# Flamingo block in one kernel: the softmax probabilities turned by VectorE and regrouped through memory in place of TensorE's transposes

## The reference

```python
x = x + jnp.tanh(g_xattn[0]) * _L0_xattn_ref(_layernorm(x, axis=-1), ctx_4096, ctx_4096, L0_xattn_Wq, L0_xattn_Wk, L0_xattn_Wv, L0_xattn_Wd)
x = x + jnp.tanh(g_ffn[0]) * _L0_ffn_ref(_layernorm(x, axis=-1), ...)
```

```python
scores = jnp.einsum('bhqd,bhkd->bhqk', queries, keys) * scale
scores = jnp.where(causal[None, None], scores, jnp.finfo(scores.dtype).min)
attn = jax.nn.softmax(scores, axis=-1)
ctx = jnp.einsum('bhqk,bhkd->bhqd', attn, values)
ctx = ctx.transpose(0, 2, 1, 3).reshape(B, Sq, NHEADS * HEAD_DIM)
return ctx @ Wd.T
```

## Time and profile before

| what | value |
|---|---|
| time, median of 3 runs | 1545.78 us (1545.67 to 1546.14) |
| the profiled execution's own time | 1548.8 us |
| its span | 1547.0 us |
| PE busy | 1480.5 us, 96% of the span |
| VectorE, ScalarE, GpSimd busy | 64%, 35%, 40% |
| chain that ended last, by engine | PE 82%, VectorE 7%, ScalarE 3%, GpSimd 3%, DMA 2% |
| a group in the middle | 79.86 us |

### The profile page before, as it was taken

One profiled execution on the slowest core, in us unless ns is written; L12 is line 12 of the kernel. 1 busy time (PEld: TensorE's weight loads), 2 busy tenths in 40 slices (PEclk: granted clock), 3 DMA queues, 4 the chain that ended last, 5 costly groups with the idle time before them and its releaser, 6 DMA issues.

```text
span 1547.0 us, 19240 instructions
## 1 busy us (share of the span) xinstructions
PE 1480.5 (96%) x7488; PEld 1214.2 (78%) x7488; DVE 990.7 (64%) x1536; ACT 537.4 (35%) x829; POOL 624.5 (40%) x403
## 2 busy tenths in 40 slices
PE   7899999999999999999999999999999999968996
PEld 7878888888888888877778888888888888855553
DVE  4956565656565656565675656464656565678995
ACT  4424131414141413144341414141413132317883
POOL 2534243434343333330443434343333333225996
PEclk9999999999999999999999999999999999998998
DMA  8823131313222222217341313121212221193553
GB/s 275 251 59 101 36 97 28 93 40 78 54 75 56 76 56 68 64 58 251 89 138 32 87 28 83 35 77 42 75 43 73 45 59 32 44 287 108 188 177 136
DMA packets 193786, 142.92 MB, mean 92 GB/s; under 512 B 147744, under 2 KB 162592, under 8 KB 193312
## 3 DMA queue, kind: packets, MB, share of 16 engines
q1 hardware_dynamic: 193264, 138.54, 31.5%
q0 software_dynamic: 432, 3.15, 1.0%
HBM read 124.88 MB, written 19.92 MB: 94 GB/s over the span
## 4 chain that ended last, share of the span: by engine, by line
PE 82%; DVE 7%; ACT 3%; POOL 3%; DMA 2%; issue 1%; SPq 1%; POOLq 0%; ACTq 0%
PE psum L511 16%; PE psum L513 16%; PE psum L512 16%; PE psum L565 7%; PE psum L600 7%; PE psum L601 7%; PE psum L602 7%; POOL go L1180 2%; PE psum L574 2%; DVE stat L1252 1%; DVE sc L1551 1%; ACT xg L1050 1%; ACT xu L1051 1%; DVE xt_lo L1208 1%; ACT xi L1055 1%
## 5 line engine op out<-in xcount | busy, mean ns | idle before, releaser
L511 PE MATMUL psum<-xt_hi,wq_hi 128*128 128x512 f32 x1024 | 405.2, 396 | 2.0 <-DVE xt_lo L1208 2.0
L513 PE MATMUL psum<-xt_hi,wq_lo 128*128 128x512 f32 x1024 | 400.1, 391 | 0.0
L512 PE MATMUL psum<-xt_lo,wq_hi 128*128 128x512 f32 x1024 | 399.4, 390 | 0.0
L1112 POOL TENSOR_TENSOR rot<-rot 128x1024 f32<-128x1024 f32 x64 | 153.5, 2399 | 430.7 <-DVE rot L1312 429.0
L1360 DVE TENSOR_TENSOR acc<-psum,acc 128x512 f32<-128x512 f32 x256 | 175.8, 688 | 164.7 <-PE psum L602 162.6
L1084 POOL TENSOR_TENSOR wd_lo<-wd_raw,wd_hi 128x512 fp32r<-128x512 f32 x128 | 164.3, 1290 | 244.6 <-ACT wd_hi L857 244.6
L511 PEld LDWEIGHTS psum<-xt_hi,wq_hi 128*128 128x128 f32 x1024 | 192.9, 188 | 41.1 <-DVE xt_lo L1208 2.8
L513 PEld LDWEIGHTS psum<-xt_hi,wq_lo 128*128 128x128 f32 x1024 | 192.5, 188 | 40.8
L512 PEld LDWEIGHTS psum<-xt_lo,wq_hi 128*128 128x128 f32 x1024 | 193.0, 188 | 38.3
L893 ACT ACTIVATE vw_hi<-psum 64x512 fp32r<-64x512 f32 x256 | 151.3, 591 | 203.6 <-PE psum L513 200.4
L1084 POOL TENSOR_TENSOR wq_lo<-wq_raw,wq_hi 128x512 fp32r<-128x512 f32 x128 | 162.3, 1284 | 139.4 <-ACT wq_hi L852 139.4
(11 more groups left out here) (130 smaller groups left out, 1964.9 us busy)
## 6 DMA issues: line engine op xcount, KB each, us to landing
wq_raw<-in_wq_t SPq DMA_DIRECT2D x128, 256.0 KB, 4.5
wd_raw<-in_wd_t SPq DMA_DIRECT2D x128, 256.0 KB, 3.1
acc<-in_x SPq DMA_DIRECT2D x16, 512.0 KB, 5.4
x_scratch<-acc SPq DMA_DIRECT2D x16, 512.0 KB, 8.1
xa<-x_scratch SPq DMA_DIRECT2D x16, 512.0 KB, 3.3
xb<-x_scratch SPq DMA_DIRECT2D x16, 512.0 KB, 4.2
xn<-in_x SPq DMA_DIRECT2D x10, 512.0 KB, 4.7
wk_raw<-in_wk_t SPq DMA_DIRECT2D x4, 1024.0 KB, 8.1
```

What stands on the lines that cost most here:

```text
L511: pe.matmul(dst, a_hi, b_hi, start=start, stop=False)
L512: pe.matmul(dst, a_hi, b_lo, start=False, stop=False)
L513: return pe.matmul(dst, a_lo, b_hi, start=False, stop=stop)
L1112: pool.tensor_tensor(rot[:, 0, :, :], rot[:, 0, :, :], rot[:, 1, :, :], ALU.add).then_inc(rope_done, 1)
```

## The change

For all units but the last two of each half (`moved`), the transposes on PE are left out. `softmax_b` ends with a transpose of `prob` in blocks of 32 by 32 on VectorE, in place. SP then stores `prob` in a scratch tensor in memory, waits for that store, and loads it back in four DMAs so that the blocks land where a whole transpose would have put them (`pt_raw`). `copy_probs` and `lower_probs` read `pt_raw`. VectorE's next subtraction into `prob` waits for the store (`p_out`) in place of PE's transposes.

```diff
+            def move_probs(unit):
+
+                n = moves(unit)
+                sp.wait_ge(turned_done, n)
+                sp.dma_start(p_dram[n % 2, :, :, :, :, :].rearrange("a q t c i -> (a q) (t c i)"),
+                             prob[:, :, :].rearrange("p s k -> p (s k)")).then_inc(p_out, 16)
+                sp.wait_ge(p_out, 16 * n)
+                if unit:
+                    sp.wait_ge(pt_lo_done, unit)
+                for c in range(4):
+                    sp.dma_start(pt_raw[32 * c:32 * c + 32, :, :, :],
+                                 p_dram[n % 2, :, :, :, c, :].rearrange("a q t i -> q t a i")).then_inc(pt_in[n % 2], 16)
...
                     if u % UPG == 3:
-                        for i in range(2, 6):
+                        for i in range(2, 5):
                             next_wd(VPG * gg + i)
+                    if u >= 1 and moved(unit - 1):
+                        move_probs(unit - 1)
+                    if u % UPG == 3:
+                        next_wd(VPG * gg + 5)
...
@@ copy_probs (ScalarE)
-                act.wait_ge(pt_ps, unit + 1)
                 if gg >= 1:
                     act.wait_ge(o_ps, (gg - 1) * OPG + (b + 1) * 2 * BT)
-                act.activation(pt_hi[:, p, b, :], p_turned, ACT.Copy).then_inc(pt_hi_done, 1)
+                if moved(unit):
+                    act.wait_ge(pt_in[moves(unit) % 2], 64 * ((moves(unit) + 1) // 2))
+                    src = pt_raw[:, :, :, :].rearrange("p t a i -> p (t a i)")
+                else:
+                    act.wait_ge(pt_ps, turns(unit))
+                    src = p_turned
+                act.activation(pt_hi[:, p, b, :], src, ACT.Copy).then_inc(pt_hi_done, 1)
...
@@ softmax_b (VectorE)
+                if moved(unit):
+                    blocks = prob[:, :, :].rearrange("p s (m k) -> p s m k", k=32)
+                    dve.wait_ge(p_done, unit + 1)
+                    dve.transpose(blocks, blocks).then_inc(turned_done, 1)
```

```diff
                     queries(unit, 2)
                     if filled:
-                        outputs(gg - 1, 0)
+                        score(unit - 1)
...
                     queries(unit, 3)
                     if filled:
-                        score(unit - 1)
                         values(gg - 1, 7)
...
                     queries(unit, 4)
                     if filled:
-                        outputs(gg - 1, 1)
+                        outputs(gg - 1, 0)
```

More of the change, by code:

```diff
@@ L91, in gated_block @@
     v_dram = nc.dram_tensor("v_scratch", (VB, P, 2, HALVES, 2, HKEYS), F32, kind="Internal").ap()
+    p_dram = nc.dram_tensor("p_scratch", (2, 4, 32, BT, 4, 32), F32, kind="Internal").ap()
     x1_dram = nc.dram_tensor("x1_scratch", (TILES, P, DIM), F32, kind="Internal").ap()
@@ L163, in gated_block @@
             acc = sb(s, "acc", [HTILES, DIM], F32)
-            kv_b = sb(s, "kv_b", [2 * KVC], F32)
+            with ExitStack() as over:
+                kv_b = sb(over, "kv_b", [2 * KVC], F32)
+            pt_raw = sb(s, "pt_raw", [BT, 4, 32], F32)
         with ExitStack() as s:
@@ L223, in gated_block @@
         pt_ps, pt_hi_done, pt_lo_done = sem("pt_ps"), sem("pt_hi_done"), sem("pt_lo_done")
+        turned_done, p_out = sem("turned_done"), sem("p_out")
+        pt_in = [sem("pt_in0"), sem("pt_in1")]
         vw_ps, vw_hi_done, vw_lo_done = sem("vw_ps"), sem("vw_hi_done"), sem("vw_lo_done")
@@ L284, in kv_bank, with moved, moves, turns @@
             return bank(S_BANK + b % 2)
+        def moved(unit):
+            return unit % UNITS < UNITS - 2
+        def moves(unit):
+            return unit + 1 - 2 * (unit // UNITS)
+        def turns(unit):
+            return unit % UNITS - (UNITS - 2) + 1 + 2 * (unit // UNITS)
         def there(n):
@@ L570, in turn_probs @@
                 pe.wait_ge(p_done, unit + 1)
-                if unit:
+                if turns(unit) > 1:
                     pe.wait_ge(pt_lo_done, unit)
@@ L608, in slot @@
                 if kind == 0:
-                    if filled:
-                        turn_probs(unit - 2)
                     queries(unit, 1)
@@ L632, in slot @@
                     if filled:
-                        outputs(gg - 1, 2)
+                        outputs(gg - 1, 1)
                     else:
@@ L638, in slot @@
                     if filled:
-                        turn_probs(unit - 2)
+                        outputs(gg - 1, 2)
                         outputs(gg - 1, 3)
@@ L905, in slot @@
                 if kind == 0 and filled:
-                    copy_probs(unit - 2)
                     copy_values(gg - 1, 6)
@@ L909, in slot @@
                     next_wq(unit, 0)
+                    copy_probs(unit - 2)
                     next_wq(unit, 1)
@@ L923, in slot @@
                 if kind == 1:
+                    next_wq(unit, 2)
+                    next_wq(unit, 3)
                     if filled:
                         copy_probs(unit - 2)
-                    next_wq(unit, 2)
-                    next_wq(unit, 3)
                     if unit > 1:
@@ L1324, in softmax_a @@
                 dve.wait_ge(max_done, unit + 1)
-                if unit:
-                    dve.wait_ge(pt_ps, unit)
+                if unit and moved(unit - 1):
+                    dve.wait_ge(p_out, 16 * moves(unit - 1))
+                elif unit:
+                    dve.wait_ge(pt_ps, turns(unit - 1))
                 dve.tensor_tensor(prob[:, :, :], view, red[:, 0, :].unsqueeze(2).broadcast_to([P, 2 * BT, KEYS]),
@@ L1343, in lower_probs @@
                 dve.wait_ge(pt_hi_done, unit + 1)
-                lower(pt_lo[:, p, b, :], p_turned, pt_hi[:, p, b, :], pt_lo_done)
+                src = pt_raw[:, :, :, :].rearrange("p t a i -> p (t a i)") if moved(unit) else p_turned
+                lower(pt_lo[:, p, b, :], src, pt_hi[:, p, b, :], pt_lo_done)
             def lower_values(gg, i):
@@ L1372, in slot @@
                         turn_second(unit - 1)
+                        lower_values(gg - 1, 6)
+                        softmax_a(unit - 1)
                         lower_probs(unit - 2)
-                        lower_values(gg - 1, 6)
-                        add(gg - 1, 0)
-                        softmax_a(unit - 1)
                         lower_values(gg - 1, 7)
@@ L1386, in slot @@
                         softmax_b(unit - 1)
+                        add(gg - 1, 0)
                         add(gg - 1, 1)
-                        add(gg - 1, 2)
                 if kind == 1:
@@ L1391, in slot @@
                     if filled:
-                        lower_probs(unit - 2)
+                        add(gg - 1, 2)
                         add(gg - 1, 3)
@@ L1397, in slot @@
                     if filled:
+                        lower_probs(unit - 2)
                         add(gg - 1, 5)
```

## The result

| | before | after |
|---|---|---|
| median of the runs, us (range) | 1545.72 (1545.10 to 1546.14) | 1667.82 (1664.71 to 1669.27) |
| ratio with its 95% interval | | 1.0788 [1.0769, 1.0806] |
| span of the profiled execution, us | 1547.0 | 1666.9 |

The change makes the kernel 7.9% slower: 122 us where 63 were forecast, and outside the range. The direction came as forecast, and so did the wait on ScalarE; each stall was longer, and the clock fell in every slot and not in a few.

What follows compares the result with a forecast made beforehand. PE was taken to bound the kernel, busy for all 79.86 us of a group. Transposes saved -26.4, stalls +77, second half's start +1.4 and clock +11.2 gave +63 us: median 1609 us, range 1578 to 1658 us.

Steps and rivals of the forecast that it cites:

- The gain: On PE, 60 of 64 units lose their four transposes, 0.44 us each: 26.4 us, all on the chain.
- Where it is late: Kind 0 slots: kind 2 unit's probabilities, copied behind late query weights on ScalarE, delay output 0; PE loses 5.5 us each.
- The rival in which the weights don't hold the copy: ScalarE could copy at once, leaving only the score's wait of 1.4 us: 1540 us, or 1519 without it; chance 0.11.
- The transpose: VectorE's transpose of 128x512 takes 0.69 us, like other operations of that shape; upper bound 1.21 us.
- Store, then wait: SP stores 256 KB of probabilities and waits 2.07 us before it can issue the loads.
- The score's wait: PE waits 1.4 us for GpSimd's sum at the score moved forward in kind 0 slots, inside the 5.5 us.
- The clock: PE's clock falls after the 4.1 us gap in 4 of 14 slots, 2.8 us each: 11 us.
- The rival with falls everywhere: The clock falls at every stall before output 0, not in 4 of 14 slots: 1637 us; chance 0.19.
- The stall's size: PE loses 5.5 us per kind 0 slot, 4.1 of them before output 0; 14 slots, 77 us.
- The 0.4 us that I added for crowding: Query weights arrive 0.4 us later because the four loads' 2048 packets crowd the DMA engines.
- the two waits at the second half's start: PE's waits for VectorE and GpSimd each grow by a transpose, 2 x 0.7 = 1.4 us.
- Regrouping slow: 128-byte pieces at 54 ns or more make copy and weights 3.5 us later: 1658 us; chance 0.07.

Runs made afterwards that it cites:

- e7: Changed kernel with query weights last on ScalarE, score and output 0 later on PE, output 0's addition earlier on VectorE in kind 0 slots: 1535.43 us, ratio 0.9931.
- e1: Changed kernel with ScalarE copying the turned probabilities before the first part of the query weights in kind 0 slots: 1601.26 us, ratio 1.0362.
- e5: Changed kernel with the probabilities' copy first and both parts of the query weights last in ScalarE's kind 0 slot: 1553.98 us, ratio 1.0051.
- e2: Changed kernel with SP loading kind 0 query weights ahead of the store and loads of the kind 2 unit's probabilities: 1604.37 us, ratio 1.0378.
- e3: Changed kernel with 22 matmuls whose product nobody reads added on PE before output 0 in each of 14 slots: 1638.12 us, ratio 1.0595.
- e9: Changed kernel with GpSimd waiting for the turned probabilities' low part before its query weights' low parts in kind 0 slots: 1658.31 us, ratio 1.0715.
- e8: Changed kernel with the four loads bringing back whole 2 KB rows, not regrouped, so probabilities land in wrong places: 1641.27 us, ratio 1.0606.

## Why the prediction was wrong

What held, step by step:

- **The gain.** 240 matmuls went, as said, and where nothing waits, a group shows it (e7: 78.50 us with 0.4 us of waits).
- **Where it is late.** The copy of the probabilities stands behind weights that SP issues late. e1 and e5 show the step on ScalarE, e2 the one on SP. The rival in which the weights don't hold the copy is refuted by these three.
- **The transpose.** 711 ns by

```profile
L1379 DVE STREAM_TRANSPOSE prob<-prob 128x512 f32<-128x512 f32 x60 | 42.7, 711 | 2.0
```

against 0.69 from the row with its shape. By the Trainium skill's table ("VectorE: DVE Perf Modes", section "The three transpose paths"), four times 311 ns, it would have been an estimated 1.24 us; this trace has 0.71, and the measurement decides.
- **Store, then wait.** 1119.27 - 1117.23 = 2.04 us, against 2.07 from the earlier trace rows. The four loads: 2.60 us against 2.44.
- **The score's wait.** 1.13 us in most slots, against 1.4.

Where it failed:

**The clock.** The prediction counted the fall in 4 of 14 slots, on the ground that 4.1 us "lies at the border" and that "Gaps of 2.59 us and less kept 1.00". That was misread in the trace of the kernel before. It has more falls than the one by the 15 us gap. This is one, behind a gap of 2.67 us at the end of the first half:

```profile
696.43 0.50 PE L600 MATMUL psum<-vw_hi,pt_hi 128*128 128x512 f32 x1 [2.67 <-DVE pt_lo L1208]
...
698.00:699.00 1.00, 1.00 (x4) 0.80 (x3) 0.94 (x3) 0.43 (x1) 1.00 (x1) 0.50 1.08 245
```

Another came behind 2.29 us, at 82.9, while 1.77 and 2.59 us at the second half's start kept the clock. So 4.1 us was well above gaps that had already lost it, and the trace gave no ground for 4 slots of 14. In the changed kernel the gaps are 4.31 us or longer, and the clock fell in all 14; in 12 of them it stood at 1.2 GHz for 6.8 us, in two for 3.4. It fell behind some shorter waits too, two of them at the score (2.05 and 1.96 us, at 142.8 and 1388.7). After the gap 13 matmuls take 1139.49 - 1133.77 = 5.72 us where 13 x 0.228 = 2.96 would do: 2.8 us, the price that I had worked out. (The 0.57 of 1403 to 1404 in the earlier trace rows puts the clock's return at 1403.9, 6.0 us behind PE's start and not 5.6, so the rows say 3.0.) The price was about right and the count wrong. e3 shows it apart from everything else: 2.1 us a slot come back with nothing changed but PE kept at work. The rest of the sum below puts all falls together at some 36 us, against 11.2. The rival with falls everywhere said 1637, and its condition was met; it missed by the stall's size.

**The stall's size.** Predicted 5.5 us, in the slot shown 1.59 + 5.96 by the profile, and 7.9 by the starts of the matmuls. It is one of the longer ones; the mean of the 14 is 1.3 + 5.6 by the profile. In the times of the slot, output 0 comes at +17.9 where +15.5 was forecast, wanted at +10.0 in both. The 2.4 us, from the rows above:

| step | predicted | measured | late |
|---|---|---|---|
| slot's start to the turned tile (low part in front, transpose) | 1.06 | 1.38 | 0.3 |
| store, wait, four loads | 4.51 | 4.68 | 0.2 |
| the Wd load's issue | 0.33 | 0.67 | 0.3 |
| weights, issue to use | 7.66 | 8.61 | 0.9 |
| weights' copy to the probabilities' copy | 0.53 | 0.54 | 0.0 |
| copy to the first output matmul | 1.37 | 2.04 | 0.7 |

The last term and a part of the first have one cause: the sentence "ScalarE's and VectorE's reads from SBUF in place of PSUM I take at nothing". The low part took 0.69 us as long as one operand came from PSUM, all 64 times in the kernel before (672 to 693 ns). With both from SBUF it takes 1.34 us when GpSimd works beside it and 0.69 when not (e2, at 1086.59; e9). The row of 1131.90 holds two of GpSimd's operations. Apart, they are

```profile
1131.90 1.27 POOL L1118 TENSOR_TENSOR wq_lo<-wq_raw,wq_hi 128x512 fp32r<-128x512 f32 x1 [8.46 <-ACT wq_hi L881]
1133.12 1.73 POOL L1118 TENSOR_TENSOR wq_lo<-wq_raw,wq_hi 128x512 fp32r<-128x512 f32 x1
```

The low part, begun at 1132.38, ends 0.55 us behind the end of the first, as if it had waited for nearly all that was left of it; the second is under way while the low part still runs, and takes 0.46 us more than the first. The shapes were equal, as the prediction says; the place of the operand was not. The kernel before has the case as well, once, among the keys' weights at the start, where both operands lie in SBUF:

```profile
58.95 2.35 DVE L1208 TENSOR_TENSOR wk_lo<-wk_raw,wk_hi 128x1024 fp32r<-128x1024 f32 x1
...
58.95 1.27 POOL L1094 TENSOR_TENSOR xn<-xn,kv_b 128x512 f32<-128x512 f32 x1
```

Without GpSimd beside it, the same operation takes 1.22 us there (at 32.57), so the term could have been read. The Trainium skill ("SBUF — State Buffer", section "🔬 SBUF: two separate sides") has the rule: a VectorE operation with two SBUF inputs and a GpSimd operation that reads SBUF lock a shared pair of ports against each other, and the later one blocks until the other is done. Trace and e9 agree with it: the low part starts 0.48 us into GpSimd's 1.27 and is held for 0.65 us.

The weights' 0.9 us are shown only in part. Over the 14 slots they take 7.8 to 9.4 us from issue to use, 8.4 on average. The 0.4 us that I added for crowding was a choice (the prediction's own 3.4 less 2.4 is 1.0), and small packets aren't its cause. In the changed kernel SP takes 4.68 us to issue the four, 3.38 before and 3.25 in e2, where they go out ahead of the store: 1.3 us of the issuing itself. Small pieces directly ahead aren't the reason (e8: 4.35 us of issuing, 8.53 to use). That the Wd block and the probabilities still in flight hold them is possible; no run here separates them.

**The rest.** The profile's idle is reckoned to a modelled end of the last matmul: 1133.77 - 1127.43 = 6.34 us between starts, less 0.228 for a matmul, is 6.11, with an idle of 5.96 shown. With the slower next start each gap costs some 0.27 us more than it shows, 8 us over 28 gaps. The first group's Wd (3.3 us) wasn't foreseen, and the two waits at the second half's start were put too low (3.00 and 4.45 us, against 1.77 and 2.59 in the earlier trace rows, so 3.1 for a forecast of 1.4).

The sum on the profiled execution: -26.4 + 81.7 (14 gaps at output 0) + 21.7 (14 at the score) + 3.5 (first group) + 3.1 (second half) leaves 36 us of 119.9 for the clock. Against the forecast's 77, that is 26 more of stall and 25 more of clock.

**Regrouping slow.** That rival said 128-byte pieces make copy and weights 3.5 us later each. e8 bounds it: without them the weights go out 1.1 us earlier, and landing takes 1.9 us in place of 2.5. A minor part of the loss.

**Unsettled:** what lengthens the weights' issue, and the last 2 us of e7.

## What to carry to other kernels

A step that is moved to another engine or through memory enters every in-order queue on its way: write down what already stands there, what it needs, and when that is due. Here late weights that nobody needed for two slots held the probabilities, and moving the weights' split to the end of the slot gave back 114 of 122 us without touching the new path; with two dates on PE and one on VectorE moved as well it became 0.7% faster than before.

Before a forecast counts on the clock, list every gap of the trace with the granted clock behind it, not the longest one alone. Here gaps of 2.3 and 2.7 us had lost it already; with a forecast of 4.1 us a slot, the fall was to be counted in all of them.

For an operation that gets its operand from SBUF in place of PSUM, look at what GpSimd does at the same time.

## What the runs showed of the hardware

- TensorE's granted clock: it fell at gaps of 4.3 to 6.7 us in front of the output in 14 of 14 slots, behind 2.29 and 2.67 us in the kernel before, which kept it at 1.77 and 2.59; matmuls of 512 columns came every 0.43 us until it was back, against 0.228. 22 idle-work matmuls in the gap made the kernel 29.7 us faster (e3).
- VectorE's 128x512 f32 operation with both inputs in SBUF: 0.69 us alone, 1.34 us beside GpSimd's subtraction of the same shape, in each of 14 slots (e9: 0.69 in each); 0.69 us with one input in PSUM, 64 times.
- VectorE's transpose of 32x32 blocks over 128x512 f32: 711 ns, against 692 for the multiplication of that shape.
- SP's issue of a 64 KB load: 0.65 us in pieces of 128 bytes, 0.43 us in rows of 2 KB (2.60 and 1.72 us for four).
- SP issues in order. With the weights first on SP (e2, 1604 us) the probabilities are late, with the probabilities first (e1, 1601 us) the weights are; only taking ScalarE's work on the weights out of the way (e5, 1554 us) ends both waits.
